# One y operation for the first half of a unit, a later y for the second half, and scale steps ahead of the rounding of x, in an fp4 feed-forward beside linear attention

## What is computed

```python
xn = layernorm(x)
# attention branch: everything about the tokens of a batch goes into one 256 x 256 matrix
Q, K, V = xn @ Wq.T + bq, xn @ Wk.T + bk, xn @ Wv.T + bv
Q, K = Q / norm(Q over tokens), K / norm(K over tokens)
tailor = 1 / (L + Q . (sum(K) + EPS))
s = xn + gamma * (sum(V) + Q.K.V) * tailor
# feed-forward branch, with blocks of 16 rounded to fp4 and back
gate, up = fp4(xn) @ fp4(w_gate).T, fp4(xn) @ fp4(w_up).T        # 256 -> 704
h = silu(gate) * up
g = silu(fp4(h) @ fp4(w_down).T)                                 # 704 -> 256
out = x + s * g
```

## Time and profile before

| | us |
|---|---|
| median of 3 runs | 593.37 (593.01 to 593.42) |
| the profiled execution | 593.2 |
| its span | 591.5 |
| TensorE matmul busy | 547.5 (93%) |
| VectorE busy | 554.6 (94%) |
| ScalarE busy | 415.6 (70%) |
| GpSimd busy | 243.4 (41%) |
| unit 2, from `h` to `h` | 14.4 |
| units 12 to 27, from `h` to `h` | 16.1 to 18.8 |

### The profile page before, as it was taken

How to read it: one execution, slowest core, us unless ns; L and a number is a source line. 1 busy time by engine, 2 the same in 40 slices (tenths; PEclk the granted TensorE clock), 3 DMA queues, 4 the chain that set the end, 5 groups by cost and what they waited for, 6 DMA issues and landing times. The chain is left out here.

```text
span 591.5 us, 15211 instructions
## 1 busy us (share of the span) xinstructions
PE 547.5 (93%) x4973; PEld 424.9 (72%) x4973; DVE 554.6 (94%) x1180; ACT 415.6 (70%) x902; POOL 243.4 (41%) x213
## 2 busy tenths in 40 slices
PE   0478999999999999999999989999999999999996
PEld 0356777778787777778787767778787777778875
DVE  6998999999999999999999997999999999987783
ACT  4979888877787787767676766777776777555431
POOL 6524433333434434434443343444343344422146
PEclk9969899999999999999999999999999999999999
DMA  8010000000011001111011111110111101103124
GB/s 253 18 37 19 19 20 19 19 20 19 19 37 37 19 2 57 55 55 55 33 44 36 54 58 56 55 36 27 49 54 55 56 37 38 37 33 129 37 95 174
DMA packets 17633, 29.15 MB, mean 49 GB/s; under 512 B 2704, under 2 KB 5136, under 8 KB 17552
## 3 DMA queue, kind: packets, MB, share of 16 engines
q1 hardware_dynamic: 17552, 28.13, 14.3%
HBM read 19.73 MB, written 8.39 MB: 48 GB/s over the span
## 5 line engine op out<-in xcount | busy, mean ns | idle before, releaser
L1495 PE MATMUL GU<-wgu,xqT 128*128 128x352 f16 x1536 | 253.7, 316 | 3.6 <-issue 2.3
L1495 PEld LDWEIGHTS GU<-wgu,xqT 128*128 128x128 f16 x1536 | 148.5, 99 | 78.2 <-issue 3.4
L564 POOL TENSOR_TENSOR ht<-h,hrr 128x1408 f32<-128x1408 f32 x32 | 82.9, 2589 | 80.2 <-DVE hrr L992 78.7
L659 ACT ACTIVATE sil<-GU,wkap 128x352 f32<-128x352 f32 x128 | 70.7, 552 | 55.7 <-PE GU L1495 54.8
L1505 PE MATMUL DS<-wdT,hqT 128*128 128x256 f16 x704 | 87.3, 272 | 0.6 <-ACT hqT L666 0.6
L523 POOL TENSOR_TENSOR xnat<-xs,xnat 128x510 f16<-128x510 f32 (+1 forms) x32 | 37.0, 1157 | 106.1 <-DVE hq L1026 89.7
L1026 DVE TENSOR_TENSOR hq<-hg,hs 128x704 f16<-128x704 f16 x128 | 79.1, 658 | 1.0
L978 DVE SCALAR_TENSOR_TENSOR h<-GU,wkap,sil 128x352 f32<-128x352 f32 x128 | 68.7, 537 | 11.6 <-ACT sil L659 8.0
L1505 PEld LDWEIGHTS DS<-wdT,hqT 128*128 128x128 f16 x704 | 66.8, 98 | 10.4 <-ACT hqT L666 0.9
L513 POOL TENSOR_TENSOR rs<-ve,half 128x2 f32<-128x2 f32 x32 | 23.8, 744 | 110.0 <-DVE ht L1015 106.1
L695 ACT ACTIVATE gring<-DS,hun 128x256 f32<-128x256 f32 (+1 forms) x64 | 29.8, 465 | 42.9 <-issue 29.1
(11 more groups left out here) (176 smaller groups left out, 954.9 us busy)
## 6 DMA issues: line engine op xcount, KB each, us to landing
xin<-in_L_attn_x SPq DMA_DIRECT2D x34, 256.0 KB, 2.8
xe<-in_L_attn_x SPq DMA_DIRECT2D x24, 256.0 KB, 2.8
out<-o SPq DMA_DIRECT2D x24, 256.0 KB, 2.0
algebra<-in_L_ffn_w_down SPq DMA_DIRECT2D x1, 704.0 KB, 7.3
gring<-in_L_ffn_w_up SPq DMA_DIRECT2D x1, 640.0 KB, 6.1
xs<-in_L_attn_x SPq DMA_DIRECT2D x2, 256.0 KB, 4.2
xt<-in_L_attn_x SPq DMA_DIRECT2D x2, 256.0 KB, 4.8
out<-xin SPq DMA_DIRECT2D x2, 256.0 KB, 2.0
```

The lines of the kernel that those rows point to most:

```text
L564: g.tensor_tensor(paired(ht[:, 0:2 * I]), paired(h[:, q]), spread(hrr[:, q], 4 * CB), ALU.mult).then_inc(S["ht_d"], 1)
L659: a.activation(sil[:, c], GU[:, c, 0, 0:CH], ACT.Silu, scale=wkap[:, 0:1]).then_inc(S["sil_d"], 1)
L1495: last = t.matmul(GU[:, c, m, 0:CH], xqT[:, k, j, 2 * a_ + kc], wgu[:, b_, kc, 2 * m + c], start=(z == 0 and kc == 0), stop=(z == 2 and kc ...
```

## The change

All of it is in the order of VectorE's calls, and in one new operation. For j = 0, except in units 18 and 26, the two `y` of 128 columns become one of 256, after `h` (0,1). For j = 1, the `y` of c = 0 moves from behind `h` (1,0) to behind the first `hq` pair (`h_round` 2), just ahead of `h` (1,1). Of the scale steps, `xss`, `xs`, `xrr` and `hs` go ahead of `x_round`; `xss` then follows `xam` and `xrr` is ahead of the rounding of h instead of behind it. The waits in the code of the other engines are the same, word for word.

```diff
@@ -1026,6 +1026,14 @@
                         v.tensor_tensor(paired(hq[:, q, j, at:at + I]), paired(hg[:, j * I:(j + 1) * I]),
                                         spread(scales[:, q, j * HB:(j + 1) * HB], HB), ALU.mult).then_inc(S[done], 1)
 
+            def e_row(p, k, j):
+                e, q, row = s_place(p, k, j)
+                halves = lambda ap: ap.rearrange("p (c n) -> p c n", c=2)
+                wait(dve, "s_d", 4 * e + 2 * row + 2)
+                wait(dve, "g_d", 2 * e + row + 1)
+                v.scalar_tensor_tensor(halves(y[:, q, row * D:(row + 1) * D]), GU[:, :, 1, CH:CH + P], unm[:, 0:1],
+                                       halves(ring(gring, e, GRING)[:, row]), ALU.mult, ALU.mult).then_inc(S["y_d"], 2)
+
             def e_half(p, k, j, c, last=False):
                 e, q, row = s_place(p, k, j)
                 n = 4 * e + 2 * row + c
@@ -1281,9 +1289,8 @@
 
                 if on["m"]:
                     h_mul(p, k, 0, 0, i)
-                if s_beside(p, 0, tail):
-                    e_half(p, k, 0, 0, last_halves(0, i))
                 if s_beside(p, 0, tail) and last_halves(0, i):
+                    e_half(p, k, 0, 0, True)
                     e_half(p, k, 0, 1, True)
                 attention(0, 0)
                 if on["xf"]:
@@ -1305,31 +1312,29 @@
                 if on["m"]:
                     h_mul(p, k, 0, 1, i)
                 if s_beside(p, 0, tail) and not last_halves(0, i):
-                    e_half(p, k, 0, 1)
+                    e_row(p, k, 0)
                 attention(0, 4)
                 if on["e"] and not on["m"]:
                     e_mul(p, k, 0)
                 if on["xa"]:
                     x_scales(p, k, 0)
                 attention(0, 2)
-                if on["xb"]:
-                    x_round(p, k, 0)
-                    x_round(p, k, 1)
-                if on["mb"]:
-                    parts(p, k, 2)
                 if on["xa"]:
                     x_scales(p, k, 1)
                 if on["xb"]:
                     x_scales(p - 1, 1 - k, 3)
+                if on["xa"]:
+                    x_scales(p, k, 2)
+                if on["mb"]:
+                    parts(p, k, 2)
+                if on["xb"]:
+                    x_round(p, k, 0)
+                    x_round(p, k, 1)
                 attention(0, 3)
                 if on["mb"]:
                     h_round(p, k, 0)
-                if on["xa"]:
-                    x_scales(p, k, 2)
                 if on["m"]:
                     h_mul(p, k, 1, 0, i)
-                if s_beside(p, 1, tail):
-                    e_half(p, k, 1, 0)
                 if on["xb"]:
                     x_round(p, k, 2)
                 if on["mb"]:
@@ -1337,6 +1342,8 @@
                 attention(1, 0)
                 if on["mb"]:
                     h_round(p, k, 2)
+                if s_beside(p, 1, tail):
+                    e_half(p, k, 1, 0)
                 if on["m"]:
                     h_mul(p, k, 1, 1, i)
                 if s_beside(p, 1, tail):
```

## The result

| | before | after |
|---|---|---|
| median of 6 runs | 593.19 (592.32 to 593.45) | 595.77 (595.38 to 596.14) |
| the profiled execution | 593.2 | 596.14 |
| its span | 591.5 | 594.4 |
| TensorE, VectorE busy | 547.5, 554.6 | 545.7, 549.1 |

The account below looks back on a forecast made before the run. TensorE and VectorE, nearly equally loaded and coupled by floating slack, bound the kernel. VectorE alone would save 3.8 us, but TensorE's gates, less what its waits give back, leave +3.4: 593.4 + 3.4 = 596.8, range 593.8 to 600.0.

Parts of the forecast that it names:

- Its sign: Whole kernel: slower, given 0.76, against 0.12 for the same and 0.12 for faster.
- the gates: TensorE's products of units 11, 19 and 27 wait for the later `y`; 2.72 us at unit 11, 3.8 with VectorE's lateness.
- its sum: Whole run: TensorE's lateness left at the end, +3.4 us on 593.4.
- (a) and (b) on VectorE: VectorE: (a) saves 0.12 us in each of 19 units, (b) 0.26 in units 10 to 28, 4.9 in all.
- The dependent pair: VectorE, units 1 to 28: `xss` directly behind `xam`, on whose result it waits, costs 0.12 us a unit.
- a trifle: VectorE: moving `xrr` adds little, making the scale steps 0.14 us a unit with the 0.12 of `xss`.
- Where small operations stand behind GpSimd: VectorE behind GpSimd's `o`: `xs` and `hs`, with two SBUF inputs, should stand in `xt`'s place; no gain counted.
- VectorE's lateness plus 2.34: Gates ahead of units 19 and 27: TensorE is late by VectorE's lateness (1.3, then 1.5) plus 2.34 us.
- That lateness is carried: TensorE between gates: no idle time to recover in, apart from few named waits, such as 0.92 us at the norms.
- The end of the run: After the last wait: the chain through TensorE and the last batch's matrices isn't shortened by the change.
- the rival put beside the forecast: Behind TensorE's stop at unit 11 the clock falls once, costing 1.7 us, carried: 598.5; 598 to 600.5 got 0.16.

Follow-up runs that it names:

- TensorE kept busy: Changed kernel plus 22 matmuls with unused results at the start of TensorE's unit 11, where it stood idle: 593.7 us, ratio to before 1.0018.
- (a): Kernel before with only the two `y` of the first half merged into one operation: 592.87 us, ratio 0.9999.
- (b): Kernel before with only the `y` of the second half, c = 0, moved behind the first `hq` pair: 593.17 us, ratio 1.0009.
- (c): Kernel before with only the scale steps moved ahead of `xt`, as in the change: 595.28 us, ratio 1.0039.
- `xrr` alone: Kernel before with only the reciprocal `xrr` moved from behind `ht` to ahead of it: 594.55 us, ratio 1.0026.
- `ham` and the whole change: Changed kernel with `ham` (block maxima of h) moved ahead of the second `hq` pair: 594.25 us, ratio to before 1.0018.

## Why the prediction came out as it did

The forecast was 596.8 with 593.8 to 600.0, slower; the time is 595.77. Its sign was right, the gates were where it put them, and its sum, +3.4 against +2.6, was fairly near. But not all terms had the right size, and that the sum came so near is in part luck. It was worked out for full clock, and the kernel with TensorE kept busy, which had full clock, ended 0.9 us later than before, at the lower edge of the range (593.7). The falls of the clock, which the forecast left out, filled the gap. Applied to one edit at a time, the same account expected +1.1, +2.0 and +0.7 to 1.3 us from (a), (b) and (c); measured were -0.1, +0.2 and +2.3. In the trace the last operation is 4.3 us late; the run began 0.35 earlier and what follows that operation took 1.0 less, which leaves the 2.9 by which the span grew.

*(a) and (b) on VectorE:* the prices were right. A merged `y` takes 0.47 to 0.49 us, 0.39 to 0.40 to the next start, and the late `y` is worth 0.26 a unit. But the 0.12 a unit of (a) mostly doesn't arrive with (a) alone: `xt`, behind `o`, swallows it, or `y` starts later. In the changed kernel `xt` never stands there (0.68 or 0.69 us in every unit), since the scale steps moved ahead of it.

*(c):* the size, 0.14 a unit and 1.1 us at unit 10, was right up to there (0.15 and 1.1; 0.08 a unit after it); its cause was half right. The dependent pair was to carry 0.12 and `xrr` "a trifle"; by the traces the pair carried 0.09 and the place of `xrr` 0.06. Yet `xrr` alone costs 1.7 us in all, and the order without any such pair took as long as that with it. The row that would have told it stood in the trace of before: `h` at 87.99 takes 0.48, at 81.57 behind the reciprocal `hrr` too, and all behind large operations 0.57 to 0.58.

*Where small operations stand behind GpSimd:* as forecast. In unit 16 of the changed kernel `hs`, 44 elements twice, takes `o`'s place for `xt` (VectorE, GpSimd):

```profile
294.65 1.28 DVE L1008 SCALAR_TENSOR_TENSOR hs<-hss,hbq,hs 128x44 f16<-128x44 f32 x2
295.86 0.68 DVE L958 SCALAR_TENSOR_TENSOR xt<-xT,xt 128x512 f32<-128x512 f32 x1
...
294.43 1.27 POOL L584 TENSOR_TENSOR o<-y,xe 128x512 f32<-128x512 f32 x1
```

The two together last 1.28 us instead of 0.34 to 0.43 and end 0.23 after `o`. The Trainium skill (SBUF — State Buffer, section "SBUF: two separate sides") says that a VectorE operation with two SBUF inputs and a GpSimd operation that reads SBUF exclude each other for the whole instruction. This trace agrees now for a small one too, which no row of before showed.

*The gates:* right. 2.72 forecast, 2.80 measured alone; 3.8 forecast with VectorE's lateness, 4.1 in the changed kernel. The stop itself is 2.81 us and not 3 to 4, since VectorE's 1.1 had reached TensorE before. At unit 19 the rule "VectorE's lateness plus 2.34" gives 2.6 + 2.34 = 4.9, and 5.1 is measured; at unit 27 5.3 and 5.4.

*That lateness is carried:* this step failed. It is carried for some units only. Of what a gate cost, TensorE gives back 1.2 to 2.1 us before the next, not 0.4 to 0.9, and 1.2 behind the last. A wait that vanishes gives back more than its recorded idle time: 1.1 for 0.92 at the norms, 0.36 for 0.19 at the last batch's matrices. Another 0.8 goes in small pieces between 249 and 257 us, mostly at the matrices of the attention branch, where the trace of before records no wait above 0.06; the gate of unit 15 takes 0.3 to 0.6 of that back. The wait for `mtop` gives back 0.8 for 0.62, but the new wait of 0.83 at the head of unit 18 takes that back too; no step of the prediction had that wait. The end then stands at VectorE's lateness at unit 26, plus 2.34, less 1.2. This rule was read off the same traces, so they don't prove it: for (b) alone it gives 0.0 and 0.0 was measured, for (a) and (b) 2.0 and 1.9, for the changed kernel 4.1 and 4.3, with TensorE kept busy 1.5 and 1.7. The last is the fair one to set beside the forecast, which was for full clock. There TensorE was 3.4, 2.9 and 1.7 us late at the gates of 19 and 27 and at the end; forecast were 3.6, 3.8 and 3.4.

*The end of the run:* the forecast took it as fixed. From the start of the last VectorE operation to the end of the span it is 2.86 to 2.95 us in all seven kernels with the merged `y`, 3.55 to 4.01 in all seven without, the kernel before among them (591.5 - 587.59). That is 0.6 to 1.1 us in favour of (a), which no step had. It lies in the last transfer of the result to memory: from the issue of the second `out<-xT` (L457) to its landing it is 1.9 us in all seven kernels with the merged `y`, and 2.6 to 3.05 in the others, 2.9 in the kernel before. Why the merged `y` should do that is open. SyncE's wait for it, in the kernel before and in that with (a) alone:

```profile
SPq L471 <- DMA out<-xT: 2.4, 1, 2.4
```

```profile
SPq L471 <- DMA out<-xT: 1.5, 1, 1.5
```

VectorE's last row, of the kernel before (span 591.5) and of that with the merged `y` alone (span 591.0):

```profile
587.59 0.43 DVE L1049 TENSOR_TENSOR xT<-G,xT 128x256 f32<-128x256 f32 x1
```

```profile
588.09 0.42 DVE L1057 TENSOR_TENSOR xT<-G,xT 128x256 f32<-128x256 f32 x1
```

*The clock:* the rival put beside the forecast, 598.5, came in part. Its fall behind unit 11 was there, and a second at the turn of the loop, where the prediction had held it off. Without the first, and in a profile without the second, the changed kernel took 593.7. So of the 2.6 us 0.9 belong to gates and scale steps at full clock, and some 1.7 to 2.1 to the lower clock. The forecast had 3.4 and 0. The parts of the two falls are known from one profile each only: about 1.6 us of TensorE's lateness came with the first, 1.0 more with the second. That the second belongs to the change is not shown. That the scale steps cost 2.3 alone and less beside (a) and (b) fits: these two make VectorE 0.26 to 0.38 us a unit earlier, which pays for the scale steps until TensorE's gates decide. Why the profiled execution of before is spared a fall at the loop and that of the changed kernel isn't, both with a stop of 2.31 us, stays open.

## What to carry to other kernels

When an operation with two SBUF inputs stands still behind one of another engine, first look for one with a single SBUF input to put ahead of it: here one exchange of two calls was worth 6.7 us. Before an operand's last reader is moved later, find who waits for that buffer: its stop can be paid with the clock as well. And the place of a small operation has a price of its own; read the durations of its successor behind both predecessors in the trace, instead of counting only what was moved.

## What the runs showed of the hardware

Behind a reciprocal of 32 or 88 elements, VectorE's `h` took 0.48 us, behind everything else, a reciprocal of 2 elements too, 0.56 to 0.58; `ht`, too, took 1.56 there instead of 1.62. A reciprocal between two large operations thus costs less than its row says.

After a stop of 2 to 2.8 us that ended in full gate/up products, TensorE's clock fell to 1.2 GHz in some traces and not in others, and the length of the stop doesn't sort them. Ahead of unit 11 it fell after 2.81 us in the changed kernel and in that with `ham` and the whole change, and after 2.65 us with (a) and (b), but not after the same 2.65 us with (b) alone. At the turn of the loop it fell after 2.14 us with (b) alone, and not after 2.51 us with `xs`, `xss` and `hs` moved. A fall cost 1.4 to 1.7 us in the one or two products behind it; with (c) alone none of that was left three units later. With TensorE fed by useless products ahead of unit 11 it stayed at 2.4 GHz, and the kernel was 1.7 to 2.1 us faster for 2.6 us more work; its profile lacks the fall at the loop too, which is part of that.

While GpSimd's `xnat` ran, a maximum over one SBUF input (`ham`) took its usual 1.61 us on VectorE, where `hq`, with two, took 1.61 instead of 0.95.
